# A chain of three recurrences and their neighbours on one core: 16-bit pair diagonals, gates seeded in PSUM, and matmuls during the tanh

## The reference, cut to what matters

```python
def step(prev_h, xw_t):                       # L0_cond: rnn
    next_h = jnp.tanh(prev_h @ Wh + xw_t)
def step(h, x_t):                             # L0_cond2: gru
    fused = jax.nn.sigmoid(jnp.concatenate([x_t, h], axis=-1) @ w_W + w_b)
    hidden_state, output_state = jnp.split(fused, 2, axis=-1)
    memory_state = x_t @ wx_W + wx_b + hidden_state * (h @ wh_W + wh_b)
    h_new = output_state * h + (1.0 - output_state) * jnp.tanh(memory_state)
def step(carry, xw_t):                        # L1_cond2: lstm
    a = xw_t + prev_h @ Wh                    # i, f, o = sigmoid, g = tanh of its quarters
    next_c = f * prev_c + i * g
    next_h = o * jnp.tanh(next_c)
```

## Time and profile before

| what | value |
|---|---|
| median of 3 runs | 8900.65 us (8898.45 to 8903.1) |
| the profiled execution | 8898.33 us |
| its span, first to last instruction | 8896.5 us |
| mean granted TensorE clock | 0.865 of full speed |
| DVE busy in the span | 7600.0 us, 85% |
| PE busy in the span | 6269.1 us, 70% |
| rnn's loop, 286 to 5404 us | 5118 us, DVE busy 4940.93 |
| gru's loop, 7551 to 7951 us | 400 us |
| lstm's loop, 8258 to 8631 us | 373 us |

### The profile page before, as it was taken

One profiled execution on the slowest core, in us unless ns is written; L12 is line 12 of the kernel. 1 busy time (PEld: TensorE's weight loads), 2 busy tenths in 40 slices (PEclk: granted clock), 3 DMA queues, 4 the chain that ended last, 5 costly groups with the idle time before them and its releaser, 6 DMA issues. The chain is left out here.

```text
span 8896.5 us, 108600 instructions
## 1 busy us (share of the span) xinstructions
PE 6269.1 (70%) x33921; PEld 2486.1 (28%) x34193; DVE 7600.0 (85%) x12570; ACT 4291.4 (48%) x4428; POOL 1329.7 (15%) x1111
## 2 busy tenths in 40 slices
PE   5677777676767676767676764488888887662779
PEld 1222222222222222222222221122222222331443
DVE  5999999999999999999999996899999997336223
ACT  3666666665656665656665663233333332112222
POOL 0000000000000000000000000377777774000000
PEclk8888888888888888888888887799999999995999
DMA  0000000000000000000000000000000000000000
GB/s 6 1 1 1 1 1 1 1 1 1 1 1 1 1 1 1 1 1 1 1 1 1 1 1 22 17 3 4 4 4 4 4 4 3 0 6 3 3 14 5
DMA packets 14002, 27.97 MB, mean 3 GB/s; under 512 B 3665, under 2 KB 11602, under 8 KB 12434
## 3 DMA queue, kind: packets, MB, share of 16 engines
q1 hardware_dynamic: 13586, 22.47, 0.9%
HBM read 15.12 MB, written 7.34 MB: 3 GB/s over the span
## 5 line engine op out<-in xcount | busy, mean ns | idle before, releaser
L901 POOL TENSOR_TENSOR hc<-hh,cg 128x512 f32<-128x512 f32 x1024 | 1296.2, 1268 | 506.9 <-DVE hh L884 506.9
L829 ACT ACTIVATE ps_m<-ps_m,aneg 128x508 f32<-128x508 f32 x1024 | 673.4, 658 | 1188.6 <-DVE hh L884 1063.5
L884 DVE TENSOR_TENSOR_SCAN hh<-ps_m,bx 128x512 f32<-128x512 f32 x1024 | 1232.9, 1209 | 0.0
L800 PE MATMUL ps_m<-hc,pick 128*128 128x512 f32 x2048 | 1051.1, 597 | 2.1 <-POOL hc L901 0.8
L508 DVE TENSOR_TENSOR_SCAN co<-rx_d 128x772 f32<-128x772 f32 x544 | 915.4, 1745 | 0.0
L508 DVE TENSOR_TENSOR_SCAN co<-rh_d 128x3088 f32<-128x3088 f32 x128 | 843.8, 6592 | 31.8 <-ACT rh_d L366 28.6
L263 PE MATMUL r_ps<-rh_diag,whq 32*128 32x512 bf16 x3072 | 360.1, 624 | 666.9 <-DVE rh_diag L127 611.5
L866 DVE TENSOR_TENSOR bx<-ps_m,bg 128x512 f32<-128x512 f32 x1024 | 675.3, 664 | 45.9 <-PE ps_m L813 45.8
L439 POOL TENSOR_TENSOR r_gate<-ident 128x1 f32<-128x1 f32 x16 | 5.7, 356 | 4576.1 <-PE r_ps L255 4576.1
L255 PE MATMUL r_ps<-wdiag,xsp 32*128 32x512 bf16 x3312 | 311.4, 528 | 517.8 <-DVE rh_gain L171 186.4
L274 PE MATMUL r_ps<-rh_diag,whn 32*128 32x512 bf16 x4608 | 438.5, 548 | 267.9 <-ACT rh_pd L395 267.9
(11 more groups left out here) (389 smaller groups left out, 11206.2 us busy)
## 6 DMA issues: line engine op xcount, KB each, us to landing
rows_scratch<-pc SPq DMA_DIRECT2D x48, 128.0 KB
rows<-rows_scratch SPq DMA_DIRECT2D x128, 48.0 KB
ew<-in_e SPq DMA_DIRECT2D x3, 1024.0 KB, 6.8
co<-in_x_dn SPq DMA_DIRECT2D x1, 1024.0 KB, 4.8
xcur<-in_x_dn SPq DMA_DIRECT2D x1, 1024.0 KB
out_x<-xcur SPq DMA_DIRECT2D x1, 1024.0 KB, 3.9
qi<-in_f_q SPq DMA_DIRECT2D x1, 384.0 KB, 3.1
xpw<-in_xp_t SPq DMA_DIRECT2D x1, 257.0 KB
```

Source lines behind the costliest of these rows:

```text
L800: e.matmul(ps[:, 6, :], pick[:, 128 - un:256 - un], hc[un % NHC][:], start=False, stop=True, skip_group_check=True).then_inc(summed, 1)
L829: e.activation(da[un % NDA][:, :, 1:T], ps[:, un % 2, :].rearrange("p (n t) -> p n t", n=NG4)[:, :, 1:T], ACT.Exp, scale=aneg[:, 0:1]).the ...
L884: e.tensor_tensor_scan(hh[un % NBUF][:], da[un % NDA].rearrange("p n t -> p (n t)"), bx[un % NBUF][:], 0.0, ALU.mult, ALU.add).then_inc(sc ...
L901: e.tensor_tensor(hc[un % NHC][:], hh[un % NBUF][:], cg[:], ALU.mult).then_inc(weighted, 1)
```

## The change

**rnn, the diagonals.** The identity has a bf16 copy `idn`, repeated for all 16 sequences. Each bf16 part of h is written twice, side by side (`part[128, 3, 16, 2]`), and the diagonal's multiplication reads the identity and the part as pairs of neighbouring 16-bit elements: both inputs and the output are bf16, and no input's innermost step is 0.

**rnn, TensorE.** After the next input product, TensorE issues twelve 128x128x512 bf16 matmuls into bank 1 (`stay_warm`), waits until 43 of the step's 51 counted DVE instructions are done (eight are left, the last being the one that writes h), and issues eight more. Nobody reads their output. In the eighth step the transpose no longer waits for ACT's copy of bank 4 to 7.

**gru and lstm.** DVE copies the next step's input parts into PSUM ("seeds" the gates) during the current step, TensorE adds its products to them (`start=False`), and ACT reads the gates from PSUM. The banks alternate by step. Products are ordered by who wants them first, each with its own count, the sigmoids are separate instructions, gru's update is computed as `old = h * upd` and `new * tanh`, and `WARM` is 5.

```diff
@@ -123,19 +123,25 @@
 
         def pieces(tl, e, F, src, dep=None):
 
+            halves = lambda x: x.rearrange("p n (a c) -> p n a c", c=2)
+
             def diagonal(q):
-                return tl.inc(e.tensor_tensor(F["diag"][:, q], id32[:].unsqueeze(1).to_broadcast([128, N, KB]),
-                                              F["part"][:, q, :].unsqueeze(2).to_broadcast([128, N, KB]), ALU.mult))
+                return tl.inc(e.tensor_tensor(halves(F["diag"][:, q]), halves(idn[:]),
+                                              F["part"][:, q].unsqueeze(2).to_broadcast([128, N, KB // 2, 2]), ALU.mult))
+
+            def cast(q, x):
+                return tl.inc(e.tensor_tensor(F["part"][:, q], x.unsqueeze(2).to_broadcast([128, N, 2]),
+                                              nought[:].unsqueeze(2).to_broadcast([128, N, 2]), ALU.add))
             if dep is not None:
                 tl.wait(dep)
-            i = tl.inc(e.tensor_tensor(F["part"][:, 0, :], src, nought[:], ALU.add))
+            i = cast(0, src)
             for q in (1, 2):
                 tl.wait(i)
-                j = tl.inc(e.tensor_tensor(F["rest"][:, q - 1, :], src if q == 1 else F["rest"][:, 0, :], F["part"][:, q - 1, :],
+                j = tl.inc(e.tensor_tensor(F["rest"][:, q - 1, :], src if q == 1 else F["rest"][:, 0, :], F["part"][:, q - 1, :, 0],
                                            ALU.subtract))
                 diagonal(q - 1)
                 tl.wait(j)
-                i = tl.inc(e.tensor_tensor(F["part"][:, q, :], F["rest"][:, q - 1, :], nought[:], ALU.add))
+                i = cast(q, F["rest"][:, q - 1, :])
             tl.wait(i)
             return diagonal(2)
 
...
@@ -305,6 +311,10 @@
             def x_mov(u):
                 return lambda b, r: wdiag[rows(b), r, N * u:N * (u + 1), :].rearrange("p m k -> p (m k)")
 
+            def stay_warm(count):
+                for _ in range(count):
+                    e.matmul(ps[:, 1, :], whq[:, 0, :], wdiag[:, 0, 0:N, :].rearrange("p m k -> p (m k)"), start=True, stop=True)
+
             def x_turn():
                 e.transpose(ps[:, 0, 0:128], xwt[:], ident[:]).then_inc(xt_mm, 1)
 
@@ -344,9 +354,11 @@
                     e.wait_ge(v, KV * t + V0 + 5)
                     product(4, xp_stat, x_mov((s + 2) % UN)).then_inc(xp_mm, 1)
                     if s == UN - 1:
-                        e.wait_ge(xa, 5 * g + 6)
                         e.wait_ge(xc, KXC * g)
                         x_turn()
+                    stay_warm(12)
+                    e.wait_ge(v, KV * t + V0 + VSUM + 36)
+                    stay_warm(8)
 
         @blk.scalar
         def _(e):
...
@@ -460,6 +472,8 @@
             for b in range(2, NB):
                 tl.wait(i)
                 i = tl.inc(e.tensor_tensor(id32[:], id32[:], ident[:, KB * b:KB * (b + 1)], ALU.add))
+            tl.wait(i)
+            tl.inc(e.tensor_copy(idn[:], id32[:].unsqueeze(1).to_broadcast([128, N, KB])))
             tl.inc(e.memset(xpc[:, :, T * N:], 0.0))
             for src, dst in ((wx[:], wxq), (wh[:], whq), (xt, xpc)):
                 n = D if dst is not xpc else T * N
...
-                e.wait_ge(warm, 1)
+                e.wait_ge(warm, 2)
                 with e.Fori(0, T // STEPS) as block:
                     for step in range(STEPS):
                         t = STEPS * block + step
-                        e.wait_ge(vec, t * KV + 1)
+                        at = 3 * (step % 2)
+                        e.wait_ge(vec, t * KV + V0)
                         h = gh[:, bass.ds(t, 1), :].rearrange("p a n -> p (a n)")
-                        for q in range(3):
-                            i = e.matmul(ps[:, q, 0:N], gw[:, 1, q * D:(q + 1) * D] if q < 2 else gwh[:], h, start=True, stop=True)
-                        i.then_inc(prod, 1)
+                        e.matmul(ps[:, at, 0:N], gw[:, 1, 0:D], h, start=False, stop=True, skip_group_check=True).then_inc(prod, 1)
+                        e.matmul(ps[:, at + 2, 0:N], gwh[:], h, start=True, stop=True).then_inc(prod, 1)
+                        e.matmul(ps[:, at + 1, 0:N], gw[:, 1, D:2 * D], h, start=False, stop=True, skip_group_check=True).then_inc(prod, 1)
                         for _ in range(WARM):
                             e.matmul(ps[:, 7, :], idle[:, 0:D], idle[:], start=True, stop=True)
 
...
-                        e.wait_ge(vec, t * KV + 2)
-                        e.activation(sg[:], gate[:], ACT.Sigmoid).then_inc(act, 1)
-                        e.wait_ge(vec, t * KV + 4)
+                        at = 3 * (step % 2)
+                        e.wait_ge(prod, t * KP + 1)
+                        e.activation(reset[:], ps[:, at, 0:N], ACT.Sigmoid).then_inc(act, 1)
+                        e.wait_ge(prod, t * KP + 3)
+                        e.activation(upd[:], ps[:, at + 1, 0:N], ACT.Sigmoid).then_inc(act, 1)
+                        e.activation(new[:], ps[:, at + 1, 0:N], ACT.Sigmoid, scale=-1.0).then_inc(act, 1)
+                        e.wait_ge(vec, t * KV + V0 + 2)
                         e.activation(th[:], r2[:], ACT.Tanh).then_inc(act, 1)
...
+                e.memset(gx[:, :, COLS:], 0.0).then_inc(warm, 1)
...
+                def seed(t, at):
+                    e.tensor_copy(ps[:, at:at + 2, 0:N], gxt[:, 0:2, bass.ds(t, 1), :].rearrange("p q a n -> p q (a n)")).then_inc(vec, 1)
...
-                        e.wait_ge(prod, t + 1)
-                        e.tensor_tensor(gate[:], ps[:, 0:2, 0:N], gxt[:, bass.ds(t, 1), 0:2, :].rearrange("p a q n -> p (a q) n"),
-                                        ALU.add).then_inc(vec, 1)
+                        at = 3 * (step % 2)
+                        e.wait_ge(prod, t * KP + 2)
                         e.wait_ge(act, t * KA + 1)
-                        e.scalar_tensor_tensor(out=r1[:], in0=ps[:, 2, 0:N], scalar=gb[:, 3:4], in1=sg[:, 0, :],
+                        e.scalar_tensor_tensor(out=r1[:], in0=ps[:, at + 2, 0:N], scalar=gb[:, 3:4], in1=reset[:],
                                                op0=ALU.add, op1=ALU.mult).then_inc(vec, 1)
-                        e.wait_ge(vec, t * KV + 3)
-                        e.tensor_tensor(r2[:], r1[:], gxt[:, bass.ds(t, 1), 2, :].rearrange("p a n -> p (a n)"), ALU.add).then_inc(vec, 1)
+                        e.wait_ge(vec, t * KV + V0 + 1)
+                        e.tensor_tensor(r2[:], r1[:], at_t(gxt[:, 2], t), ALU.add).then_inc(vec, 1)
+                        seed(t + 1, 3 - at)
                         e.wait_ge(act, t * KA + 2)
-                        e.tensor_tensor(r3[:], at(gh, t), th[:], ALU.subtract).then_inc(vec, 1)
-                        e.wait_ge(vec, t * KV + 5)
-                        e.tensor_tensor(r4[:], r3[:], sg[:, 1, :], ALU.mult).then_inc(vec, 1)
-                        e.wait_ge(vec, t * KV + 6)
-                        e.tensor_tensor(gh[:, bass.ds(t + 1, 1)].rearrange("p a n -> p (a n)"), r4[:], th[:], ALU.add).then_inc(vec, 1)
+                        e.tensor_tensor(old[:], at_t(gh, t), upd[:], ALU.mult).then_inc(vec, 1)
+                        e.wait_ge(act, t * KA + 4)
+                        e.tensor_tensor(r4[:], new[:], th[:], ALU.mult).then_inc(vec, 1)
+                        e.wait_ge(vec, t * KV + V0 + 5)
+                        e.tensor_tensor(at_t(gh, t + 1), r4[:], old[:], ALU.add).then_inc(vec, 1)
 
...
-                        e.wait_ge(vec, t * KV + 1)
+                        at = 2 * (step % 2)
+                        e.wait_ge(vec, t * KV + V0)
                         h = lh[:, bass.ds(t, 1), :].rearrange("p a n -> p (a n)")
-                        for q in range(4):
-                            i = e.matmul(ps[:, q, 0:N], lwh[:, q * D:(q + 1) * D], h, start=True, stop=True)
-                        i.then_inc(prod, 1)
+                        for q, bank, lo in ((0, 0, 0), (1, 0, N), (3, 1, N), (2, 1, 0)):
+                            i = e.matmul(ps[:, at + bank, lo:lo + N], lwh[:, q * D:(q + 1) * D], h, start=False, stop=True,
+                                         skip_group_check=True)
+                            if q in (1, 2):
+                                i.then_inc(prod, 1)
                         for _ in range(WARM):
                             e.matmul(ps[:, 7, :], idle[:, 0:D], idle[:], start=True, stop=True)
...
-                        e.wait_ge(vec, t * KV + 2)
-                        e.activation(s3[:], gate[:, 0:3, :], ACT.Sigmoid).then_inc(act, 1)
-                        e.activation(gg[:], gate[:, 3, :], ACT.Tanh).then_inc(act, 1)
-                        e.wait_ge(vec, t * KV + 5)
+                        at = 2 * (step % 2)
+                        e.wait_ge(prod, t * KP + 1)
+                        e.activation(keeps[:].rearrange("p a n -> p (a n)"), ps[:, at, 0:2 * N], ACT.Sigmoid).then_inc(act, 1)
+                        e.wait_ge(prod, t * KP + 2)
```

(59 more changed lines are left out.)

## The result

The changed kernel takes 8859.93 us, the median of 20 runs from 8794.2 to 8925.61; the kernel before, 8904.15 us (20 runs, 8889.69 to 8915.56). The ratio is 0.9948, with a 95% interval of 0.9931 to 0.9966: 0.5% faster, where 2.4% were forecast. The runs of the changed kernel also spread over 131 us, those of before over 26.

A forecast was written before the change was run, and what follows sets the result against it. rnn was held bound by a chain over one step, DVE tightest, TensorE's way as long and its clock falling; gru and lstm by latency. Sum: 8898.3 - 96 (diagonals) + 49 (clock) - 109 (gru) - 56 (lstm) = 8686 us, range 8550 to 8785.

The forecast's parts named there:

- The step that failed: gru and lstm: one idle matmul less a step is covered by the wait for h, so it costs nothing.
- The term of 109 + 56 = 165 us: gru and lstm: shorter steps gain 0.85 us a step (109 us) in gru and 0.44 (56 us) in lstm.
- The rival of half latencies: gru and lstm gain half as much, as seeds, extra sigmoids and register instructions stand on the chain: 8766 us, chance 0.10.
- gru's own terms: gru's step: 0.74 us less to the reset gate, 0.2 less between tanh and h, 0.1 back; net given as 0.85.
- Their latencies themselves: gru and lstm: loops of about 291 and 317 us after the change, from shorter chains in each step.
- Diagonals: rnn: three multiplications of about 420 ns instead of 687, net 0.75 us a step, 96 us in all.
- Twenty matmuls: rnn: they speed up the product, cost the path nothing, and move the clock's fall ahead of L281; net +49 us.
- the forecast's -47: rnn's whole change: the diagonals' -96 us with +49 us for the moved low clock.
- The low stretches that go: rnn: today's low clock over L281, put at 0.64 us a step, is removed: -82 us.
- The new low stretches: rnn: the clock falls ahead of L281 in 0.6 of the steps, at 1.7 us each: 1.0 us a step.
- The rival in which the clock stays up: rnn: the rests hold the clock and low stretches over L281 are gone: 8555 us, chance 0.25.
- The slower rival: rnn: the twenty matmuls at low clock delay the product, each step losing 3.05 us less 0.2 slack: 9098 us, chance 0.05.

The follow-up runs named there:

- e1: The changed kernel with WARM = 6 instead of 5 in gru and lstm, nothing else: 8654.81 us, ratio 0.9714.
- e2: The kernel before with WARM = 5 instead of 6, nothing else: 9084.94 us, ratio 1.0202.
- e4: The kernel before with gru and lstm changed and WARM = 6, rnn as before: 8713.12 us, ratio 0.9787.
- e3: The kernel before with rnn alone changed (pair diagonals and twenty matmuls), gru and lstm as before: 8831.15 us, ratio 0.9919.
- e11: e7 with the old diagonals again (f32 identity, single 16-bit parts): 8684.87 us, ratio 0.9754.
- e7: e1 plus seven filling matmuls ahead of rnn's residue and eight behind it: 8603.14 us, ratio 0.9661.
- e8: e1 plus eight filling matmuls behind rnn's residue only: 8706.25 us, ratio 0.9776.
- e6: The kernel before with the twenty matmuls alone in rnn, old diagonals, gru and lstm as before: 8992.58 us, ratio 1.0098.
- e5: The kernel before with the pair diagonals alone in rnn, no added matmuls, gru and lstm as before: 8860.12 us, ratio 0.995.

## Why the prediction was wrong

**The step that failed** is the one on `WARM`, which was put at nothing: "One matmul of idle work less is covered by the wait for h", because "six products' passes and five matmuls (0.7 + 1.1) still fit". It asked only whether five matmuls fit beside the chain, and not what they were there for. The term of 109 + 56 = 165 us gained came out, in the profiled execution, as 22 - 83 = 61 us lost. e1 and e2 show it from both sides: with six, the seeded kernel takes 8654.81 us; with five, the old one takes 9084.94. The argument about the clock was made for rnn alone; gru and lstm stood at 9 tenths before, and I took that as given. The rival of half latencies named the right loops and the wrong reason. (gru's own terms, 0.74 + 0.2 - 0.1, add to 0.84 and not 0.85, which changes nothing.)

**Their latencies themselves were right, and a little better than forecast.** At the full clock gru's step is 2.22 us and lstm's 2.39 us (forecast 2.3 and 2.49), and e4 gives -192 us for the two where 165 were forecast. ACT reads a 128x16 gate from PSUM in 0.18 us, where I had used 0.2 to 0.23. The Trainium skill's rule in "VectorE: DVE Perf Modes", section "The TRN2 errata — SBUF-src ops pay a fixed extra latency per instruction" (a smaller fixed cost from PSUM), agrees with the 0.18 against the 0.23 of the earlier trace rows, though the old instruction also had twice the elements. The changed kernel's trace has both sources at one size, 0.22 us for the tanh of `r`, which is in SBUF, and 0.18 for the sigmoid of a gate in PSUM, though they are different functions:

```profile
7500.13 0.22 ACT L1035 ACTIVATE th<-r 128x16 f32<-128x16 f32 x1 [0.22 <-DVE r L1059]
7501.41 0.18 ACT L1030 ACTIVATE reset<-ps_g 128x16 f32<-128x16 f32 x1 [1.07 <-PE ps_g L1013]
```

**Diagonals: right in duration, and somewhat high in worth** (82 us at a held clock, where 96 were forecast). The group that answers to L127 of the earlier trace rows:

```profile
L129 DVE TENSOR_TENSOR rh_diag<-idn,rh_part 128x512 bf16<-128x512 bf16 x387 | 162.8, 421 | 6.0
```

421 ns, forecast 422. This row agrees with the Trainium skill, "Vector Engine (DVE) Microarchitecture Reference", section "Performance modes — why throughput varies by op and dtype" (two elements a cycle if every operand is 2 bytes wide with an innermost step of one). The identity's type and the pairs were changed together, so no run tells which of the two conditions the old instruction missed. The step after one such diagonal, in the timeline of the changed kernel, answers to the earlier trace rows:

```profile
2944.34 1.90 PE L316 MATMUL r_ps<-wdiag,whq 128*128 128x512 bf16 x8 [0.18 <-DVE tq L218]
...
2946.29 1.60 PE L269 MATMUL r_ps<-rh_diag,whq 32*128 32x512 bf16 x24
...
2947.02 0.43 DVE L129 TENSOR_TENSOR rh_diag<-idn,rh_part 128x512 bf16<-128x512 bf16 x1
...
2947.92 2.07 ACT L407 ACTIVATE rh_pd<-r_ps 128x512 f32<-128x512 f32 x4 [2.11 <-PE r_ps L269]
2950.05 2.12 PE L280 MATMUL r_ps<-rh_diag,whn 32*128 32x512 bf16 x36 [2.15 <-ACT rh_pd L407]
...
2954.49 5.40 PE L287 MATMUL r_ps<-rh_s,negid 128*128 128x512 f32 x8 [2.32 <-DVE rh_s L515]
```

**Twenty matmuls: right in kind, and near in number by luck.** The eight are done when the first diagonal is, the product takes 1.60 us instead of 2.75, ACT's copy starts 0.47 us behind the third diagonal (forecast 0.4), the rest ahead of L287 is 2.32 us instead of 1.68 (forecast 2.4), and L287 takes 5.40 us: the fall has moved there, as forecast. The mean step is 5053.6 / 127 = 39.79 us, forecast 39.9; e3's -73 us stand against the forecast's -47. But that -47 was the sum of three terms, and each of them was too large.

- *The diagonals*, -96 us: e11 against e7 says -82.
- *The low stretches that go*, 0.64 us a step or -82 us: e11 differs from e4 by the filling matmuls alone, apart from a copy and a wait, holds the clock with the old diagonals, and is 28 us faster. The 0.64 was what was left of 0.84 us behind an estimate of 0.20 for the turn, measured from the single step of 39.46 us. In the trace of before the steps across a turn took 43.57 us in the mean and the others 39.86, so the turn makes up (43.57 - 39.86) / 8 = 0.46 us, and L281's first group took over 5 us in only 7 of the 112 steps inside the passes.
- *The new low stretches*, 0.6 x 1.7 us a step or +131 us: 39 of the 112 steps were hit, not 0.6 of them, and at 40.49 us against 38.94 in the others, 1.55 us each.

So rnn's mean came out 0.1 us from its forecast because a gain and a loss were both overstated. The rival in which the clock stays up was wrong for this kernel. In e7, with fifteen more matmuls and six idle ones, no step inside a pass is over 40 us; the two terms by which that rival differs from the forecast are 131 us, and e7 is 52 us faster than e1.

**The slower rival** (the twenty matmuls hold up the product) did not happen in rnn. But the same mechanism, idle matmuls at the low level ahead of wanted ones, is what happened in gru and lstm; in e8 idle matmuls stood ahead of wanted ones too, though at the full clock. I had priced it in one place and not looked for the others.

**Open.** Why the clock fell in gru at 7559.7 and in lstm at 8191.2 and not a step earlier or later was not tested. The 20 runs' times go with their mean clocks, and with six idle matmuls the spread shrinks to 19 us, so the spread comes from how long gru and lstm run at the low level; but where the clock fell is known for the profiled execution alone.

## What to carry to other kernels

Before idle matmuls that hold the clock are made fewer, the smaller number has to be tried by itself; that they fit beside the chain says nothing of the clock. In gru and lstm, old and new, the clock fell at five a step and held at six, and in the new kernel 205 us lie between the two. Idle matmuls stand in TensorE's list like all others, so at the low clock they delay what they were meant to speed up, and a loop can stay in that state; read the granted clock of every stretch that has them, not of the slowest stage alone. Filling one of two neighbouring rests can be worse than filling neither (e8): the clock fell in the other one, the work behind it ran late, and the filling behind that held up wanted matmuls although it ran at the full clock itself. And a mean that comes out as forecast proves none of its terms; here three were off and cancelled.

## What the hardware showed that was not expected

TensorE busy all the time did not bring the clock back: 435.00 us of 435 busy, clock 0.50. Nor does the busy share sort the loops. gru of the changed kernel, with five idle matmuls a step, was busy for 56.23 us of 65 just before it fell, and gru of before, with six, kept 1.00 with 274.36 us of 408 busy:

```profile
7545.00:7953.00 408.00, 274.36 (x1510) 151.24 (x1540) 144.37 (x769) 69.63 (x268) 0.00 (x0) 1.00 0.00 0
```

The Trainium skill, "TensorE: Matmul & The Clock Gate", section "Part 1: The HAM clock gate (the "warmup" mystery)", says that the clock is set by how busy TensorE has been. By busy time as these rows measure it, in which the ends of matmuls are modelled, this case does not bear that out. What the clock does follow was not tested by itself.

Three more things were not expected:

- A spread of 131 us over 20 runs of one program on one core. With one idle matmul more a step the spread was 19 us over 5 runs.
- A turn of rnn's loop cost 3.8 us with eight steps written out and 5.0 us with sixteen.
- In rnn, the same twenty matmuls cost 85 us with the old diagonals (e6) and earned 25 us with the new ones (e3 against e5).
